# A causal solve of 128 rows per tile: three hops of 32 rows for seven of 16

## The chip, the cores and the metric

The kernel runs on 1 core of a Trainium2 chip. The metric is device time in microseconds (us), measured outside the profile. A profiled execution gives the trace, and has a time of its own.

## The reference, cut to what matters

The whole kernel computes four layers on x[4, 512, 128]: a selective scan, an attention with a mixture of experts, the causal layer below, and attention with experts again. The change touches the causal layer alone (16 heads of 8 columns, 4 sequences of 512 rows):

```python
logits = jnp.einsum('bhqd,bhkd->bhqk', q, k) * scale
probs = jax.nn.softmax(logits + causal_mask, axis=-1)
L = jnp.eye(s, dtype=probs.dtype) - jnp.tril(probs, -1)
rhs = jnp.diagonal(probs, axis1=-2, axis2=-1)[..., None] * v
A = jax.scipy.linalg.solve_triangular(L, rhs, lower=True)
return A.transpose(0, 2, 1, 3).reshape(b, s, HID) @ Wd.T + bd
```

For each head a lower triangular system of 512 rows is solved with 8 right sides. Row i of A needs all the rows before it.

## The kernel before, in words

`delta_phase` (L1459) is the causal layer. It goes over 16 tiles of 128 rows, n = 0 to 15 (4 sequences of 4 tiles), one after the other, since tile n needs the rows solved in the tiles before it in its sequence. A tile's solve has these parts:

- `from_earlier` (L2302) multiplies the solved rows of earlier tiles with the off-diagonal exponentials. With the tile's own right side that gives `g_nat`.
- Before that, POOL inverts the 128 diagonal blocks of 16x16 (8 blocks of rows by 16 heads, one block per partition) in `inverse_block` (L1700): one product with 1/sum (L1704), 28 small products and adds (L1710, L1715), the unit (L1718), a last product (L1722, `xz_blk`).
- SP carries data around for this, in `inverses` (L1776), `blocks_out` (L1757) and `sums_out` (L1767). `blocks_out(n)` writes the 8 diagonal blocks of the exponentials to DRAM with 8 DMAs (L1761), waits for them and loads them as `e_blk`, one block per partition (L1765). `sums_out(n)` does the same for the row sums (L1769, L1774); DVE takes their reciprocal `zi_blk` (L2042), which releases POOL. `inverses(n)` waits for POOL's last step, stores `xz_blk` (L1778), waits, and loads it with 8 DMAs into block-diagonal place, `xT` (L1785).
- PE multiplies exponentials and inverses (`multiplied`, L2244, four groups of 4 heads, 128x128x128 each), and ACT copies the result to `mT` (L1853).
- The solve: `inverse` (L2315) applies the inverses to `g_nat`, and then seven turns of 16 rows, k = 1 to 7, in two halves of 8 heads each: `product` (L2319) of the rows solved so far with `mT`, DVE adds 16 columns to `aT` (L2120), PE transposes `aT` back (L2293, `turned`), and ACT copies it to `a_nat` (L1890). `output` (L2295) multiplies with Wd, and DVE adds to x (L2090).

Every engine runs a program in order, and the order is written out by hand. In iteration n of the outer loop (n = -6 to 15) the turns of tile n are taken, and between them stand 14 places, h = 0 to 13, at which `beside(n, h)` does work for later tiles: at these **hooks** the maxima of tile n+3 or n+4 (up to 2 groups per hook), the scores and exponentials of tile n+3, the sums of tile n+2 (column at h = 3, reciprocal at h = 7), the products for `mT` of tile n+1 (h = 9 to 12, MT_HOOKS). At the start of a sequence the hooks also do its rotation and splitting into bf16 parts (h = 0 to 6 of the iteration four tiles ahead), and SP stores these parts and loads the operands `q_op` and `k_op` (L1740, L1746, L1748; 1152 KB and three times 384 KB). For the first tile of a sequence the scores stand at h = 10 to 13, otherwise from h = 0.

SP's order in iteration n is: `inverses(n+1)`, `blocks_out(n+2)`, `sums_out(n+2)`, `shifts` (maxima, L1750), and where a new sequence comes, the parts and the operands:

```python
if in_program(n + 1):
    inverses(n + 1)
if in_program(n + 2):
    blocks_out(n + 2)
    sums_out(n + 2)
```

So the work of POOL on tile n+2 is released at h = 7 of iteration n, and its result goes to SP at the head of iteration n+1.

## Time and profile before

| what | value |
|---|---|
| median of 3 runs | 1795.72 us (1794.52 to 1796.07) |
| profiled execution, its own time | 1797.81 us |
| its span in the profile | 1795.7 us |
| mean granted TensorE clock | 0.82 |
| PE / DVE / ACT / POOL busy | 74% / 60% / 42% / 31% |
| causal layer in the trace | about 788 to 1388 us |

Busy shares are averages over four layers with different limits. In a timeline row the first number is the start in us from the span's start, the second the time until the last of the merged instructions has ended; SPq is SP's queue, where a duration is that of issuing, not of the transfer. "x16" counts instructions. An fp32 matmul stands as two records (PE) with two weight loads (PEld), a transpose as one. A row of a table of stretches holds its two ends, its length, the busy us and instructions (x) of PE, PEld, DVE, ACT and POOL, then PEclk (the granted TensorE clock, 1 is 2.4 GHz), the DMA share and GB/s. Brackets at a row's end give the engine's idle time before it and what ended it.

### The profile page before, as it was taken

The page shows a single profiled execution, that of the slowest core. Times are in us where ns is not written, and L with a number is a line of the kernel's source. Part 1 is how long each engine was busy: PE and PEld are TensorE (multiplying, and loading weights), DVE is VectorE, ACT ScalarE, POOL GpSimd, SP SyncE. Part 2 cuts the span into 40 slices and gives each one's busy share as a digit, 9 for nine tenths or more (in the row PEclk, how much of TensorE's full clock was granted, in tenths as well). Part 3 has the DMA queues.
Part 4 walks back from the last instruction along what each step waited for, and adds up shares of the span by engine and source line. Part 5 has one row for each costly group of instructions (what it writes and reads, how often), then busy time and mean ns, then how long its engine had stood idle before and what let it go on. Part 6 is the DMA issues. An engine that isn't in the chain of part 4 may idle for free. (4 is left out here: it accounts for less than half of the span.)

```text
span 1795.7 us, 31360 instructions
## 1 busy us (share of the span) xinstructions
PE 1336.6 (74%) x11698; PEld 690.8 (38%) x11698; DVE 1084.9 (60%) x2290; ACT 760.3 (42%) x1622; POOL 559.0 (31%) x782
## 2 busy tenths in 40 slices
PE   2646666655999986733788988988978589999855
PEld 1212222221223222731465666765656212322255
DVE  2789899966878762533645635635512587886143
ACT  2445444420366675521342443433422016566734
POOL 1266556632122111530332422422331321310133
PEclk9659899985699998875687976977977569999968
DMA  8600000003233100213141141141110222410012
GB/s 258 221 0 1 0 0 0 0 3 92 51 102 114 42 9 6 63 37 71 20 86 26 16 90 22 18 88 22 21 21 8 74 72 59 151 49 9 6 48 74
DMA packets 118060, 92.03 MB, mean 51 GB/s; under 512 B 85855, under 2 KB 108959, under 8 KB 116735
## 3 DMA queue, kind: packets, MB, share of 16 engines
q1 hardware_dynamic: 115422, 84.99, 18.9%
q0 software_dynamic: 2496, 5.13, 0.9%
q8 instruction: 91, 1.49, 0.4%
q14 instruction: 51, 0.42, 0.1%
HBM read 69.55 MB, written 38.36 MB: 60 GB/s over the span
## 5 line engine op out<-in xcount | busy, mean ns | idle before, releaser
L980 DVE TENSOR_REDUCE f_row_min<-f_ps 128x1 f32<-128x512 f32 x512 | 335.6, 681 | 113.3 <-PE f_ps L1272 107.5
L874 ACT ACTIVATE f_e<-f_ps 128x512 f32<-128x512 f32 x512 | 289.0, 601 | 219.9 <-PE f_ps L1297 210.3
L1272 PE MATMUL f_ps<-f_operands 72*128 72x512 bf16 x512 | 229.1, 452 | 60.6 <-DMA f_operands<-k_scr 24.0
L1297 PE MATMUL f_ps<-f_operands 75*128 75x512 bf16 x512 | 191.3, 393 | 7.9 <-ACT f_e L874 7.9
L260 POOL TENSOR_TENSOR m_drive<-m_du,m_b_row 128x1024 f32<-128x1024 f32 x64 | 154.2, 2414 | 98.2 <-ACT m_b_row L309 95.5
L1272 PEld LDWEIGHTS f_ps<-f_operands 72*128 72x128 bf16 x512 | 51.8, 102 | 278.8 <-DVE f_row_min L980 221.4
L417 DVE TENSOR_TENSOR_SCAN m_h<-m_ps,m_drive 128x512 f32<-128x512 f32 x128 | 149.1, 1206 | 3.4 <-POOL m_drive L260 3.4
L1981 DVE TENSOR_REDUCE d_row_min<-d_ps 128x1 f32<-128x384 f32 (+3 forms) x176 | 106.3, 634 | 68.0 <-PE d_ps L2186 67.2
L1308 PE MATMUL f_ps<-f_e,f_v_op 128*32 128x512 f32 x1024 | 141.1, 624 | 1.4 <-ACT f_e L874 1.4
L517 PE MATMUL m_ps<-m_hC,sb_ident 128*128 128x512 f32 x256 | 126.0, 615 | 5.6 <-DVE m_hC L426 5.6
L2120 DVE TENSOR_TENSOR d_aT<-d_ps,d_aT 128x16 f32<-128x16 f32 x224 | 37.7, 168 | 140.7 <-PE d_ps L2288 140.4
L1890 ACT COPY d_a_nat<-d_ps 128x64 f32<-128x64 f32 x224 | 47.8, 213 | 165.8 <-PE d_ps L2293 165.1
L494 PE MATMUL m_ps<-m_bc,sb_pick 96*128 (+1 forms) x128 | 50.8, 407 | 88.8 <-DVE m_hC L426 72.4
L2183 PE MATMUL d_ps<-d_k_op,d_q_op 72*128 72x128 bf16 (+3 forms) x256 | 77.7, 377 | 46.9 <-DMA d_k_op<-k_scr 28.0
L2293 PE MATMUL d_ps<-sb_ident,d_aT 128*128 128x128 f32 x256 | 90.1, 354 | 28.9 <-DVE d_aT L2120 26.6
L1704 POOL TENSOR_TENSOR d_xT_blk<-d_e_blk,d_zi_blk 128x256 f32<-128x256 f32 x16 | 13.2, 828 | 256.8 <-DVE d_zi_blk L2042 256.8
L309 ACT COPY m_b_row<-m_ps 128x512 f32<-128x512 f32 x64 | 37.5, 586 | 128.5 <-PE m_ps L494 128.5
L2250 PE MATMUL d_ps<-d_xT,d_e_nat 128*128 128x128 f32 x512 | 89.1, 330 | 1.4 <-ACT d_e_off L1848 1.4
L313 ACT ACTIVATE m_ps<-m_delta,m_A 128x512 f32 x128 | 83.6, 689 | 2.7 <-DVE m_h L417 2.2
L2250 PEld LDWEIGHTS d_ps<-d_xT,d_e_nat 128*128 128x128 f32 x512 | 81.4, 241 | 4.1 <-issue 3.0
L2288 PE MATMUL d_ps<-d_mT,d_a_nat 32*32 32x16 f32 (+6 forms) x3584 | 77.4, 195 | 4.4 <-ACT d_a_nat L1890 3.9
L760 POOL DMA_INDIRECT f_rows_scr<-f_h2n,f_place_u x32 | 32.5, 1015 | 153.8 <-DVE f_place_u L1104 146.4
(250 smaller groups left out, 2407.2 us busy)
## 6 DMA issues: line engine op xcount, KB each, us to landing
f_rows_scr<-blank SPq DMA_DIRECT2D x2, 8707.5 KB, 42.2
f_wall<-f_wall SPq DMA_DIRECT2D x2, 4624.0 KB
f_operands<-q_scr SPq DMA_DIRECT2D x32, 288.0 KB
f_operands<-k_scr SPq DMA_DIRECT2D x96, 96.0 KB
d_q_op<-q_scr SPq DMA_DIRECT2D x4, 1152.0 KB
d_k_op<-k_scr SPq DMA_DIRECT2D x12, 384.0 KB
q_scr<-f_part SPq DMA_DIRECT2D x24, 128.0 KB, 2.3
k_scr<-f_part SPq DMA_DIRECT2D x24, 128.0 KB, 2.4
```

The costliest lines, as they stand in the source:

```text
L260: nc.gpsimd.tensor_tensor(drive[:, n % AHEAD, :, :], du[:, :, now], b_row[:, n % AHEAD, :].unsqueeze(1).to_broadcast([P, HALVES, S]), ALU. ...
L313: last = nc.scalar.activation(ps[:, DECAY + HALVES * (n % 2) + k, :], delta[:, k, now], ACT.Exp, scale=A[:, k, n:n + 1])
L417: last = nc.vector.tensor_tensor_scan(h[:, n % 2, k, :], ps[:, DECAY + HALVES * (n % 2) + k, :], drive[:, n % AHEAD, k, :], 0.0, ALU.mult, ...
L517: last = nc.tensor.matmul(ps[:, Y + k, :], core.ident[:, :], hC[:, n % 2, k, :], start=(n == 0), stop=(n == N_STATE - 1))
L874: nc.scalar.activation(e_sb[:, n % 3, hh, :], ps[:, SCORE[u % SCORE_BANKS], :], ACT.Exp, scale=SCALE).then_inc(s["e_out"], 1)
L980: nc.vector.tensor_reduce(row_min[:, b % 2, u // TPB, u % TPB:u % TPB + 1], ps[:, MAXQ[u % MAX_BANKS], :], AX.X, ALU.max, negate=True).the ...
L1272: nc.tensor.matmul(ps[:, MAXQ[u % MAX_BANKS], :], q_op(b, QK)[:, hd, t * P:(t + 1) * P], k_op(b, QK)[:, hd, :], start=True, stop=True).the ...
L1297: nc.tensor.matmul(ps[:, SCORE[u % SCORE_BANKS], :], k_op(b, QKS)[:, hd, t * P:(t + 1) * P], q_op(b, QKS)[:, hd, :], start=True, stop=True ...
L1308: last = nc.tensor.matmul(ps[hh * HEAD_COLS:(hh + 1) * HEAD_COLS, O_BANK, :], v_of(b, t, g * GROUP + hh), e_sb[:, n % 3, hh, :], start=(t ...
L1981: nc.vector.tensor_reduce(row_min[:, n % 2, g * heads:(g + 1) * heads], dve_bank("maximum", n, g)[:, 0:heads * cols].rearrange("p (h c) -> ...
L2250: last = nc.tensor.matmul(bank[:, hh * P:(hh + 1) * P], e_nat[:, n % 3, hd, :], xT[:, n % 2, hd, :], start=True, stop=True)
L2293: nc.tensor.transpose(turn_bank(half), src[:, half, :], core.ident[:, :]).then_inc(done, 1)
```

## The change

- The solve goes in three hops of 32 rows (HOP, `product`, `turned`, `added`). The sums are transposed back and added in natural order straight into `a_all`; DVE does the adds, ACT copies the products `uT`.
- The inverse of a block of 32 is joined from two of 16 on PE: `paired` at h = 5 (64 matmuls of 32x32x32, 16 heads by 4 blocks), DVE masks, `joined` at h = 7 (64 more), DVE adds: `yT`. `mT` is built from `yT` in three groups at h = 9, 10, 11, of 16 matmuls with 32 rows and 32, 64 or 96 weight columns.
- For this POOL writes the inverses in two orders (one more product of 128x256), and SP loads them with 16 DMAs for 8. `e_blk` has two buffers, and `blocks_out` is done one tile earlier: after `sums_out`, and for the first tile of a sequence as the last thing of SP's iteration.
- The output leaves the solve: POOL packs `a_all` into `a_out` at the head of the next iteration, PE transposes it at h = 1, ACT copies, PE multiplies once at h = 3, DVE adds to x there. The loop has one more iteration.
- Constants: `d_wd` in half the size, `pair_mask` of 32 columns for `off_blocks` of 128, fewer and smaller memsets.

```diff
-HOOKS = 2 * TURNS
+HOP = 32
+HOPS = P // HOP
+LAST_HOP = HOPS - 1
+HOOKS = 14
+PAIR_HOOK, JOIN_HOOK = 5, 7
+TURN_OUT, OUTPUT = 1, 3
-MT_HOOKS = (9, 10, 11, 12)
+MT_HOOKS = (9, 10, 11)
...
             @block.gpsimd
-                nc.gpsimd.memset(xT[:, :, :, :], 0.0).then_inc(s["set"], 1)
+                nc.gpsimd.memset(xp[:, :, :, :, :], 0.0).then_inc(s["set"], 1)
...
-                    nc.gpsimd.tensor_tensor(xz_blk[:, :, :], xT_blk[:, :, :],
+                    nc.gpsimd.tensor_tensor(xz_blk[:, 0, :, :], xT_blk[:, :, :],
                                             zi_blk[:, :].unsqueeze(2).to_broadcast([P, BLK, BLK]),
                                             ALU.mult).then_inc(s["blk_step"], 1)
+                    nc.gpsimd.tensor_tensor(xz_blk[:, 1, :, :], xT_blk[:, :, :].rearrange("p c i -> p i c"),
+                                            zi_blk[:, :].unsqueeze(1).to_broadcast([P, BLK, BLK]),
+                                            ALU.mult).then_inc(s["blk_step"], 1)
+
+                def packed(n):
+                    pool.wait_ge(s["a_sb"], 2 * HOPS * (n + 1))
...
+                    for half in range(2):
+                        nc.gpsimd.tensor_copy(by_group(a_out[:, heads_of(half), :]),
+                                              own_cols(a_all[:, n % TPB, :], half)).then_inc(s["a_packed"], 1)
...
             @block.sync
-                    if n >= 1:
-                        sp.wait_ge(s["blk_step"], BLK_STEPS * (n - 1) + 1)
-                    sp.dma_start(e_blk[:, :, :], e_scr[n].rearrange("k h i j -> (k h) i j")).then_inc(s["e_in"], 16)
+                    if n >= 2:
+                        sp.wait_ge(s["blk_step"], BLK_STEPS * (n - 2) + 1)
+                    sp.dma_start(e_blk[:, n % 2, :, :], e_scr[n].rearrange("k h i j -> (k h) i j")).then_inc(blocks_in(n), 16)
...
                     for k in range(BLKS):
-                        own = slice(k * BLK, (k + 1) * BLK)
-                        sp.dma_start(xT[own, n % 2, :, own], x_scr[n, k].rearrange("h c i -> c h i")).then_inc(s["x_in"], 16)
+                        own, cols = slice(k * BLK, (k + 1) * BLK), slice(k % 2 * BLK, (k % 2 + 1) * BLK)
+                        for form in range(2):
+                            sp.dma_start(xp[own, n % 2, form, :, cols], x_scr[n, k, :, form].rearrange("h r c -> r h c")).then_inc(
+                                s["x_in"], 16)
...
                     if in_program(n + 2):
-                        blocks_out(n + 2)
                         sums_out(n + 2)
+                    if in_program(n + 3) and (n + 3) % TPB:
+                        blocks_out(n + 3)
                     if in_program(n + 3) and (n + 3) % TPB == 0:
                         shifts(n + 3)
...
                     if in_program(n + 4) and (n + 4) % TPB != 0:
                         shifts(n + 4)
+                    if in_program(n + 3) and (n + 3) % TPB == 0:
+                        blocks_out(n + 3)
...
             @block.scalar
+                def hop_out(n, k):
...
+                    own = slice(k * HOP, (k + 1) * HOP)
+                    for half in range(2):
+                        act.wait_ge(s["u_ps"], u_done(n, k, half))
+                        nc.scalar.copy(uT[:, half, own], ps[:, STEP[half], own]).then_inc(s["u_sb"], 1)
...
             @block.vector
+                def paired(n):
+                    dve.wait_ge(s["dve_ps"], in_dve("pair", n))
+                    nc.vector.tensor_tensor(pair[:, :, :], dve_bank("pair", n).rearrange("p (h i) -> p h i", h=NH),
+                                            w["pair_mask"].unsqueeze(1).to_broadcast([P, NH, HOP]), ALU.mult).then_inc(s["dve_out"], 1)
+
+                def joined(n):
+                    dve.wait_ge(s["dve_ps"], in_dve("join", n))
...
+                    nc.vector.tensor_tensor(yT[:, n % 2, :, :], dve_bank("join", n).rearrange("p (h i) -> p h i", h=NH),
+                                            xp[:, n % 2, 0, :, :], ALU.add).then_inc(s["dve_out"], 1)
...
+                for n in range(-LEAD, TILES_N + 1):
...
+                    if in_program(n):
+                        first_rows(n)
+                    for h in range(3, 6):
+                        beside(n, h)
+                    added(n, 1)
+                    for h in range(6, 9):
+                        beside(n, h)
+                    added(n, 2)
...
             @block.tensor
+                def in_blocks(bank, lhs, rhs):
+                    for hd in range(NH):
+                        for b in range(HOPS):
+                            rows = hop_rows(b)
+                            last = nc.tensor.matmul(bank[rows, hd * HOP:(hd + 1) * HOP], lhs(rows, hd), rhs(rows, hd),
+                                                    start=True, stop=True)
+                    last.then_inc(s["dve_ps"], 1)
+
+                def paired(n):
+                    pe.wait_ge(s["x_in"], 16 * 2 * BLKS * (n + 1))
+                    in_blocks(dve_free("pair", n), lambda rows, hd: e_nat[rows, n % 3, hd, rows],
+                              lambda rows, hd: xp[rows, n % 2, 0, hd, :])
...
+                    rows = hop_rows(i + 1)
+                    for hd in range(NH):
+                        last = nc.tensor.matmul(bank[0:(i + 1) * HOP, hd * HOP:(hd + 1) * HOP],
+                                                e_nat[rows, n % 3, hd, 0:(i + 1) * HOP], yT[rows, n % 2, hd, :],
                                                 start=True, stop=True)
...
+                def product(n, k):
...
+                    own, rows = slice(k * HOP, (k + 1) * HOP), slice(0, k * HOP)
+                    pe.wait_ge(s["act_out"], in_act("mt", n, k - 1))
+                    for half in range(2):
+                        pe.wait_ge(s["a_sb"], a_done(n, k - 1, half))
+                        side_by_side(half, a_all[:, n % TPB, :], lambda hd: mT[rows, n % 2, k - 1, hd, :], rows, own, s["u_ps"])
...
+                    beside(n, 4)
+                    product(n, 1)
+                    beside(n, 5)
+                    turned(n, 1)
+                    beside(n, 6)
+                    beside(n, 7)
+                    product(n, 2)
+                    beside(n, 8)
+                    turned(n, 2)
+                    beside(n, 9)
+                    beside(n, 10)
+                    product(n, 3)
+                    beside(n, 11)
+                    turned(n, 3)
```

In `inverse(n)` the 16 matmuls of 128x128 become 64 of 32x32 by 8 columns, all into one bank; DVE copies them to `a_all` (`first_rows`).

## Rows read from the trace of the kernel before

**Rows 1.** Lines L1704, L1722 and the longest wait for a DMA, causal layer.

```profile
L1704 POOL TENSOR_TENSOR d_xT_blk<-d_e_blk,d_zi_blk x16: 822/827/838, 865.8 to 1341.6; 128x256 f32<-128x256 f32 x16
L1722 POOL TENSOR_TENSOR d_xz_blk<-d_xT_blk,d_zi_blk x16: 622/622/625, 877.5 to 1352.9; 128x256 f32<-128x256 f32 x16
DVE d_zi_blk L2042 <- DMA d_z_blk<-z_scr: 41.5, 10, 7.3
```

**Rows 2.** Timeline, 1294 to 1313 us, SP's queue and POOL.

```profile
1294.75 0.62 POOL L1722 TENSOR_TENSOR d_xz_blk<-d_xT_blk,d_zi_blk 128x256 f32<-128x256 f32 x1
1295.40 0.34 SPq L1778 DMA_DIRECT2D x_scr<-d_xz_blk  x1
1297.11 4.50 SPq L1785 DMA_DIRECT2D d_xT<-x_scr  x8
1301.66 3.91 SPq L1761 DMA_DIRECT2D e_scr<-d_e_nat  x8
1307.80 0.34 SPq L1765 DMA_DIRECT2D d_e_blk<-e_scr  x1
1308.18 0.43 SPq L1769 DMA_DIRECT2D z_scr<-d_zT  x1
1310.05 0.34 SPq L1774 DMA_DIRECT2D d_z_blk<-z_scr  x1
1311.93 0.83 POOL L1704 TENSOR_TENSOR d_xT_blk<-d_e_blk,d_zi_blk 128x256 f32<-128x256 f32 x1 [16.56 <-DVE d_zi_blk L2042]
```

**Rows 3.** Stretches from one L1704 to the next: length, engines' busy time, PEclk, DMA.

```profile
894.00:922.00 28.00, 23.24 (x359) 18.28 (x359) 16.49 (x39) 15.57 (x38) 9.69 (x31) 0.74 0.15 22
922.00:959.00 37.00, 30.05 (x485) 21.83 (x485) 13.30 (x43) 6.94 (x25) 9.65 (x31) 0.68 0.49 102
959.00:989.00 30.00, 26.64 (x449) 19.69 (x449) 17.34 (x60) 12.26 (x33) 10.80 (x32) 0.87 0.14 21
989.00:1021.00 32.00, 30.10 (x547) 21.06 (x548) 20.02 (x58) 14.30 (x39) 11.19 (x33) 1.00 0.14 21
1049.00:1088.00 39.00, 31.24 (x485) 22.54 (x485) 13.32 (x43) 7.03 (x26) 9.64 (x31) 0.68 0.47 97
1088.00:1119.00 31.00, 28.12 (x443) 20.54 (x444) 17.40 (x58) 11.90 (x32) 10.70 (x32) 0.78 0.14 21
```

**Rows 4.** Timeline of SP's queue, 1048 to 1080 us: a sequence's operands.

```profile
1055.01 0.88 SPq L1746 DMA_DIRECT2D d_q_op<-q_scr  x1
...
1061.43 0.35 SPq L1778 DMA_DIRECT2D x_scr<-d_xz_blk  x1
1073.25 3.75 SPq L1785 DMA_DIRECT2D d_xT<-x_scr  x8
```

**Rows 5.** Landing of L1785; products on PE; L1942 and L2288 (ns, min/median/max).

```profile
DMA to landing us min/median/max: 1.6/1.9/3.7
...
1005.15 0.31 PE L2288 MATMUL d_ps<-d_mT,d_a_nat 16*32 16x16 f32 x16
...
L1942 DVE TENSOR_TENSOR d_v_raw<-d_ps,sb_rows x4: 691/692/692, 801.7 to 1132.4; 128x512 f32<-128x512 f32 x4
...
L2288 PE MATMUL d_ps<-d_mT,d_a_nat x3584: 177/183/238, 903.5 to 1385.5; 16*32 16x16 f32 x29, 48*32 48x16 f32 x29, 80*32 80x16 f32 x29, 112*32 112x16 f32 x29
...
1024.39 1.06 PE L2250 MATMUL d_ps<-d_xT,d_e_nat 128*128 128x128 f32 x8
```

**Rows 6.** Timeline of ACT, 1093 to 1101 us: the last exponential of tile 8.

```profile
1099.89 0.60 ACT L1843 ACTIVATE d_e_nat<-d_ps 128x512 f32<-128x512 f32 x1 [0.20 <-PE d_ps L2206]
```

**Rows 7.** Timeline of the layer's start: memsets.

```profile
788.28 3.51 POOL L1685 MEMSET d_xT<- 128x4096 f32 x1 [11.68 <-POOLq L2386]
793.66 0.22 DVE L1912 MEMSET d_unit_blk<- 128x1 f32 x16 [3.87 <-POOL d_a_all L1686]
```

**Rows 8.** Timeline of DVE in the last tile: second halves of turns 3 and 4.

```profile
1378.89 0.17 DVE L2120 TENSOR_TENSOR d_aT<-d_ps,d_aT 128x16 f32<-128x16 f32 x1 [0.20 <-PE d_ps L2288]
1380.14 0.17 DVE L2120 TENSOR_TENSOR d_aT<-d_ps,d_aT 128x16 f32<-128x16 f32 x1 [0.20 <-PE d_ps L2288]
```

**Rows 9.** Groups by line, 870 to 1400 us: weight loads of the turns' transposes, idle before.

```profile
L2293 PEld LDWEIGHTS d_ps<-sb_ident,d_aT 128*128 128x128 f32 x256 | 40.0, 156 | 52.0 <-DVE d_aT L2120 35.5 <-DVE d_aT L2114 8.5 <-issue 3.1
```

More of the change, by code:

```diff
@@ L2063, in beside @@
                         maximum(m, g)
+                    if in_program(n + 1) and h == PAIR_HOOK:
+                        paired(n + 1)
+                    if in_program(n + 1) and h == JOIN_HOOK:
+                        joined(n + 1)
                     for m, g in block_sums_in(n, h):
@@ L2123, in _ @@
[L2123 to L2133 removed]
+                        own, target = (by_group(t[:, heads_of(half), :]) for t in (vn[:, n % 4], g_nat))
@@ new lines, in added @@
+                def added(n, k):
+                    if not in_program(n):
+                        return
+                    own = slice(k * HOP, (k + 1) * HOP)
+                    for half in range(2):
+                        target = own_cols(a_all[:, n % TPB, :], half)[own]
+                        dve.wait_ge(s["un_ps"], u_done(n, k, half))
+                        if k == 1:
+                            dve.wait_ge(s["a_sb"], a_done(n, 0, half))
+                        nc.vector.tensor_tensor(target, turned_cols(half)[own], target, ALU.add).then_inc(s["a_sb"], 1)
@@ new lines, in paired, with joined @@
+                def paired(n):
+                    pe.wait_ge(s["x_in"], 16 * 2 * BLKS * (n + 1))
+                    in_blocks(dve_free("pair", n), lambda rows, hd: e_nat[rows, n % 3, hd, rows],
+                              lambda rows, hd: xp[rows, n % 2, 0, hd, :])
+                def joined(n):
+                    pe.wait_ge(s["dve_out"], in_dve("pair", n))
+                    in_blocks(dve_free("join", n), lambda rows, hd: xp[rows, n % 2, 1, hd, :],
+                              lambda rows, hd: pair[rows, hd, :])
@@ L2361, in _, with inverse @@
-                output(TILES_N - 1)
+                def inverse(n):
+                    pe.wait_ge(s["gn_sb"], 2 * (n + 1))
+                    pe.wait_ge(s["dve_out"], in_dve("join", n))
+                    for hd in range(NH):
+                        for b in range(HOPS):
+                            rows = hop_rows(b)
+                            last = nc.tensor.matmul(a0_bank()[rows, hd * HD:(hd + 1) * HD], yT[rows, n % 2, hd, :],
+                                                    g_nat[rows, hd, :], start=True, stop=True)
+                    last.then_inc(s["a0_ps"], 1)
```

306 lines of the change are left out of this document (160 added, 146 removed).

## The prediction

> **What bounds the kernel now.** The page's busy shares say nothing about the causal layer, so I first read its lines. POOL starts a tile's inverses 16 times, from 865.8 to 1341.6 us [rows 1]: 15 intervals, 31.7 us in the mean. The list of waits then tells what that start waits for: POOL always for DVE's reciprocal, and DVE in 10 of 16 cases for the DMA that brings the sums, for 41.5 us together [rows 1]. A DMA that a fast engine waits for again and again is the end of a chain, so I followed one on SP's queue [rows 2]. POOL ends a tile at 1295.37; SP stores its result and waits until 1297.11 (1.74 us), issues 8 loads (4.50), 8 stores of the next tile's blocks, waits for them and loads them (6.5 from 1301.66 to 1308.18), sends the sums there and back (1.87, then 1.88 until POOL starts). That is 16.56 us. POOL itself takes 12.0 (1341.6 to the end of the last L1722 at 1353.5 [rows 1]). The ring POOL, SP, POOL has 28.5 us, and intervals of 28 us stand in the table of stretches [rows 3]. **It is a ring of one POOL and one SP queue, not the seven turns, that paces most tiles.** PE is busy for 23 of those 28 us.
>
> The long intervals confirm it. In those of 37 to 39 us (three) the DMA share is 0.47 to 0.49 [rows 3]: a sequence's operands are issued at 1055.01, and the small store behind them, issued at 1061.43, lets SP go on at 1073.25 only [rows 4]. Only where PE is busy for 30.1 of 32 us at full clock (989 to 1021 [rows 3]) does PE pace; I count three such intervals.
>
> **What the change does to that ring.** Each interval is the longest of three paths; I price the two that it touches.
>
> POOL: one more product of 128x256. The two such products take 0.62 and 0.83 [rows 1]; it reads transposed, as the 0.83 does, so POOL takes 12.8.
>
> SP: 16 loads for 8. Eight took 4.50 and 3.75 [rows 2, 4], so 16 take 7.5 to 9.0; I take 8.7, since these stretches come now and then. The last lands 1.9 after its issue [rows 5]. From POOL's end to the inverses in place: 1.74 + 8.7 - 0.45 + 1.9 = 11.9 us.
>
> The sums no longer stand behind the blocks: 1.74 + 8.7 + 1.87 + 1.88 = 14.2 for 16.56. With POOL that path is 27.0, 1.5 less than now.
>
> But `paired` waits on PE for those loads at h = 5, while the products for `mT` waited at h = 9 to 12. Behind it on PE stand hooks 5 to 13, and DVE behind PE, with the reciprocal of h = 7 that starts POOL. That closes a **second ring**: POOL 12.8, SP 11.9, and from there to h = 7. The pair: a small product of 16 records takes 0.31 [rows 5], of which 0.18 is one record's own time (the median of L2288 [rows 5]), so about 0.13 for 16 starts, 0.032 for four records on four groups of columns. 128 records are 32 such rounds, 1.0 us, and 1.2 with the tail. DVE's mask from PSUM: 0.69, as L1942 of that shape [rows 5]. Two adds of 64 columns, 0.45. That and the signals make 2.8 us until POOL starts. With two maxima of 0.7 at h = 6: 4.2. Where a sequence's split stands at h = 5 and 6 (two subtractions of 1024 columns, and ACT's cast between them): 6.1. I have no row for the split as a whole; 5 to 7 bounds it, three times. The ring is 27.5, 28.9 or 30.8.
>
> **The 15 intervals.**
> - The first: 28.9 for 28, +1.
> - Three with the split (as 894 to 922, two of 28 and one of 30 [rows 3]): 30.8 for 28.9, +6 together.
> - Three with operands: SP reaches them 4.3 later (8 more loads), POOL's start has moved by 1.5 (18.0 for 16.56 after its end), so 2.8 later against it; behind the landed store 8.7 - 0.45 + 1.9 + 4.2 = 14.4 follows for 15.1 before (1073.25 to 1088.4). +2.1 each, +6.
> - Three behind a new sequence's first scores (as 959 to 989 and 1088 to 1119 [rows 3]): here `blocks_out` of that tile is now SP's last step, and waits for exponentials at h = 13, with the next `inverses` queued behind. The last ended at 1100.49 [rows 6], 12.1 after POOL's start at 1088.4, so POOL's result, ready at 12.8, waits until 12.1 + 6.5 = 18.6. Then 11.9 and 4.2: 34.7 for 30.6. +4.1 each, +12.
> - Three that PE paces: 0. PE's work grows and shrinks alike: pair, join and the 64 small matmuls of `inverse` are 3 x 1.0 where `inverse` was 0.9; `mT` has 96 records with 32, 64 or 96 weight columns. Eight records of L2250 with 128 weight columns take 1.06 [rows 5], of which about 0.27 is the last one's tail, so 0.11 each; by weight columns, 32 records each of 96, 64 and 32 take 2.7 + 1.8 + 0.9 = 5.4 for 3.6 (32 of 128). Against this 16 transposes fall to 6 and 14 products to 6; a pair with its gaps is some 0.4, -3.9 together.
> - The last two, without maxima: 27.5 for 29, -3.
>
> Sum: **+22 us**. From the last start of POOL to the layer's end: inverses in place 5.0 later; then pair and join with their DVE steps (4.0) and longer `mT` (1.8) against turns that no longer stand between (-2.7); then four turns fewer in the last tile, 1.25 each (1378.89 to 1380.14 [rows 8]), and small steps, -5.3 with the longer way out over POOL in it. +2.8. At the start, DVE waits 3.87 us for POOL's memsets; that of 4096 columns, 3.51 us, becomes half [rows 7]: -1.8.
>
> Costed at nothing: ACT has 10 copies fewer and one more per tile, and is not last anywhere in [rows 2]. The output's packing on POOL stands before the next tile's inverses, in 16 us of idle time [rows 2]; if that cover went it would be 0.6 per tile. DVE's adds fall from 14 to 6, but pair and join are two of 0.69: even. Smaller constants: 0.1 MB of the first load, at most 0.4 us.
>
> Total 22.3 + 2.8 - 1.8 = +23.3 on an execution of 1797.8 us (span 1795.7), 2.1 above the median of the runs. On that median: 1795.7 + 23.3 = **1819 us**.
>
> **A price the trace doesn't hold.** In this trace no product of the causal layer has rows that begin above partition 0; the four column groups of L2288 run side by side, 16 records in 0.31 us [rows 5]. `in_blocks` puts four row groups after each other, into one bank. If those ran one after the other, 128 records would take 4.1 instead of 1.0; if they overlap more, nothing is gained on the ring beyond 1 us. I take 1.0, the row that is nearest. The Trainium skill (TensorEngine Tiling (Array Packing), Restrictions and Gotchas) says that different row tiles cannot access the same PSUM bank simultaneously; by that rule the first of the two holds, and the sum would be that of rival 1. No run here shows it yet.
>
> **Rivals.**
> 1. Row groups take turns (13%). Pair +3.1 on the second ring in 12 intervals, 37 us, and three times 3.1 in the tail: +46, **1865 us**. For it: nothing in the trace. Against it: the column groups overlap.
> 2. The turns pace, not the ring (18%): **faster**. If the inverses land before PE comes to h = 5, `paired` waits for nothing, and what counts are round trips. PE's weight loads stood idle for 52.0 us ahead of the turns' transposes [rows 9]; four of seven turns gone saves 30: **1766 us**. Place: PE at h = 5; it decides where PE's way from h = 7 to the next h = 5 is over 24.7 us. For it: PE is busy for 30 us in several stretches. Against: only 23 of 28 in others, and the 41.5 us of waits for the sums.
> 3. The second ring at its lower bounds (10%): 16 loads in 7.5 and 1 us less from pair to h = 7 take 2.2 from each of 11 intervals, 24 us: **1795 us**, no change.
> The change could also fail to shorten the solve at all; that is in the forecast already, since hops are not on the ring.
>
> **How the numbers follow.** The forecast has 59%. About 0.2% (3.6 us) is what a measurement of this kernel can tell from no change. Rival 2 lies below that, rival 3 on both sides of it. Faster 0.21, same 0.05, slower 0.74. The range reaches from just above rival 2 to just above rival 1, 1770 to 1872; the forecast's own, by its bounds (7.5 to 9.0, 5 to 7, exponentials 2 us earlier or later), is 1800 to 1840.
>
> **What would show it.** PE idle ahead of `paired`, ended by the DMA into `xp`, 2 to 5 us in most tiles; starts of L1704's successor 27 to 31 us apart, 34 to 35 three times, 39 to 42 three times; DVE's reciprocal no longer waiting for its DMA. `paired` and `joined` 1.2 us long at full clock, over 4 if rival 1 holds. I am wrong if PE shows no idle time there, or if the ordinary intervals fall below 27 us.

## The result, and the profile after

The changed kernel takes **1935.88 us** in the median of 4 runs (1935.27 to 1948.57); the kernel before took 1795.88 (4 runs) beside it. The ratio is 1.0798, 95% interval 1.0754 to 1.0843: slower by 140 us, where +23 was forecast. The sign was right, the size was six times too small, and the range given was 1770 to 1872.

The profiled execution has a span of 1934.1 us for 1795.7, and the 138 us between them all lie in the causal layer. From the first start of POOL's product to the layer's last addition it took 522 us and takes 660. The stretch over the whole layer, first of the kernel before, then of the changed one (columns as in [rows 3]: length, busy time of PE, PEld, DVE, ACT, POOL, granted clock, DMA):

```profile
866.00:1388.00 522.00, 444.05 (x7611) 326.18 (x7609) 243.08 (x740) 190.05 (x543) 160.74 (x501) 0.81 0.21 37
```

```profile
866.00:1527.00 661.00, 558.32 (x12045) 449.61 (x12043) 259.56 (x645) 153.56 (x384) 178.37 (x549) 0.64 0.21 36
```

PE's busy time rose by 114 us, and it runs 12045 matmul records for 7611; the forecast had PE's work even. The granted clock fell from 0.81 to 0.64 of full speed, which the forecast did not ask about.

POOL's chain and the way of the sums are what the forecast said: POOL's last product takes 0.83 us, for 0.62 [rows 1], and DVE's reciprocal no longer waits for its DMA (41.5 us before [rows 1], 0.6 now). The lines of the changed kernel, then its list of waits in the layer:

```profile
L1731 POOL TENSOR_TENSOR d_xT_blk<-d_e_blk,d_zi_blk x16: 821/823/846, 866.2 to 1464.7; 128x256 f32<-128x256 f32 x16
L1752 POOL TENSOR_TENSOR d_xz_blk<-d_xT_blk,d_zi_blk x16: 822/826/844, 878.3 to 1476.6; 128x256 f32<-128x256 f32 x16
```

```profile
POOL d_xT_blk L1731 <- DVE d_zi_blk L2098: 263.5, 16, 26.9
ACT d_mT L1898 <- PE d_ps L2361: 185.2, 48, 11.1
...
PE d_ps L2342 <- DMA d_xp<-x_scr: 25.6, 9, 5.2
...
PE d_ps L2418 <- issue: 14.4, 9, 2.4
PE d_ps L2342 <- issue: 12.2, 8, 2.8
...
DVE d_zi_blk L2098 <- DMA d_z_blk<-z_scr: 0.6, 1, 0.6
```

POOL, which starts a tile, now waits 263.5 us for DVE, DVE waits for PE, and ACT waits 185.2 us for the products of `mT` (L2361). PE waits for the inverses (L2342 is the matmul of pair and join) in 9 of 16 tiles only. So PE paces most tiles, not the second ring. Two rows "issue" are new: PE idle inside its own streams, for nothing that the profile shows.

The stretches between two starts of POOL that answer to [rows 3]:

```profile
895.00:927.00 32.00, 30.15 (x667) 25.02 (x669) 17.54 (x35) 11.20 (x25) 9.95 (x32) 0.61 0.21 31
927.00:968.00 41.00, 33.27 (x767) 27.79 (x760) 14.05 (x38) 6.89 (x20) 10.82 (x35) 0.62 0.46 96
968.00:1016.00 48.00, 39.10 (x746) 30.38 (x743) 18.79 (x54) 10.39 (x24) 11.95 (x36) 0.57 0.15 22
1016.00:1061.00 45.00, 39.69 (x819) 30.73 (x818) 22.22 (x52) 11.88 (x28) 12.30 (x36) 0.73 0.15 22
```

The third was 30 us long with PE busy for 26.6 at clock 0.87, the fourth 32 at full clock. PE's timeline in one tile shows where its time went:

```profile
1067.52 1.91 PE L2361 MATMUL d_ps<-d_yT,d_e_nat 32*32 32x32 f32 x32
1069.67 3.62 PE L2361 MATMUL d_ps<-d_yT,d_e_nat 32*64 32x32 f32 x32
1073.81 5.32 PE L2361 MATMUL d_ps<-d_yT,d_e_nat 32*96 32x32 f32 x32
1091.28 1.93 PE L2342 MATMUL d_ps<-d_xp,d_e_nat 32*32 32x32 f32 x128
```

`mT` takes 1.91 + 3.62 + 5.32 = **10.85 us** in every tile; the forecast had 5.4. The pair's 128 records take 1.93 us in most tiles, at a granted clock of 0.5 (1.2 GHz), and 1.29 in the few that fall in a time of full clock, as the last tile's join:

```profile
1429.00 1.93 PE L2342 MATMUL d_ps<-d_xp,d_e_nat 32*32 32x32 f32 x128
1433.10 1.29 PE L2342 MATMUL d_ps<-d_pair,d_xp 32*32 32x32 f32 x128
```

The forecast had 1.2 (1.0 and a tail), and 4.1 in place of the 1.0 if the row groups took turns. They run side by side, and rival 1 is false. The Trainium skill (TensorEngine Tiling (Array Packing), Restrictions and Gotchas) says that different row tiles cannot access the same PSUM bank simultaneously. Here four of them write one bank at once, each into partitions of its own, at 1.29 us / 128 = 10 ns per record; the measurement decides.

Last, SP's queue behind a new sequence's first scores. POOL's last product starts at 979.82 and takes 0.82:

```profile
978.65 0.69 SPq L1795 DMA_DIRECT2D d_q_op<-md_scr  x1
991.68 3.74 SPq L1801 DMA_DIRECT2D e_scr<-d_e_nat  x8
996.67 0.34 SPq L1805 DMA_DIRECT2D d_e_blk<-e_scr  x1
997.05 0.43 SPq L1818 DMA_DIRECT2D x_scr<-d_xz_blk  x1
```

POOL's result is stored 16.4 us after its end; the forecast had 5.8, by the same mechanism, since the exponentials that SP waits for came 12.1 us after POOL's start and now come 24.

### The profile page after: what moved, and what is told of

Its sections match the earlier page's. It is cut to its first block and busy times, and to the rows that moved or that the text cites. A ratio compares the mean times of both kernels' runs of the same rounds, so it can differ in the third digit from the quotient of the medians.

```text
span 1934.1 us, 40328 instructions
## 1 busy us (share of the span) xinstructions
PE 1451.3 (75%) x16130; PEld 814.1 (42%) x16130; DVE 1099.9 (57%) x2193; ACT 723.3 (37%) x1462; POOL 574.3 (30%) x830
## 5 line engine op out<-in xcount | busy, mean ns | idle before, releaser
L2361 PE MATMUL d_ps<-d_yT,d_e_nat 32*32 32x32 f32 (+2 forms) x1536 | 173.3, 290 | 1.6 <-ACT d_e_off L1892 1.1
L2361 PEld LDWEIGHTS d_ps<-d_yT,d_e_nat 32*32 32x32 f32 (+2 forms) x1536 | 167.3, 215 | 11.1 <-issue 6.6
L2274 PE MATMUL d_ps<-d_k_op,d_q_op 72*128 72x128 bf16 (+3 forms) x256 | 82.6, 395 | 38.9 <-DMA d_k_op<-k_scr 28.8
L2202 DVE TENSOR_TENSOR d_a_all<-d_ps,d_a_all 32x64 f32<-32x64 f32 x96 | 19.1, 220 | 146.7 <-PE d_ps L2423 145.7
L1898 ACT COPY d_mT<-d_ps 32x512 f32<-32x512 f32 (+2 forms) x48 | 27.7, 578 | 185.2 <-PE d_ps L2361 185.2
L1731 POOL TENSOR_TENSOR d_xT_blk<-d_e_blk,d_zi_blk 128x256 f32<-128x256 f32 x16 | 13.2, 827 | 263.5 <-DVE d_zi_blk L2098 263.5
L426 DVE TENSOR_TENSOR m_hC<-m_h,m_ps 128x1024 f32<-128x1024 f32 x64 | 78.1, 1221 | 2.1
L494 PEld LDWEIGHTS m_ps<-m_bc,sb_pick 96*128 96x128 bf16 x128 | 12.5, 100 | 150.8 <-DVE m_hC L426 115.6
```

Of the source, the lines that this page charges most:

```text
L2274: nc.tensor.matmul(bank[:, hh * cols:(hh + 1) * cols], q_op[0:QK_ROWS, hd, rows_of(t)], k_op[0:QK_ROWS, hd, 0:cols], start=(hh == 0), stop ...
L2361: last = nc.tensor.matmul(bank[0:(i + 1) * HOP, hd * HOP:(hd + 1) * HOP], e_nat[rows, n % 3, hd, 0:(i + 1) * HOP], yT[rows, n % 2, hd, :], ...
```

## The experiments

All in one table first; the intervals are means over the kind of tile that the forecast priced, between starts of POOL's first product, with the tail from the last start to the layer's end.

| us | first | 3 split | 3 operands | 3 late blocks | 3 PE-paced | last 2 | tail | whole kernel |
|---|---|---|---|---|---|---|---|---|
| before | 28.3 | 29.0 | 37.9 | 30.6 | 32.3 | 29.1 | 46.1 | 1795.9 |
| forecast | 28.9 | 30.8 | 40.0 | 34.7 | 32.3 | 27.5 | 48.9 | 1819 |
| changed | 28.4 | 35.7 | 40.9 | 47.8 | 43.5 | 33.2 | 61.3 | 1935.9 |
| e1_cols | 28.3 | 35.0 | 42.3 | 40.9 | 38.3 | 30.7 | 56.0 | 1887.5 |
| e13_few_codes | 28.4 | 32.8 | 38.4 | 38.9 | 35.6 | 28.8 | 48.7 | 1848.6 |
| e17_few_hooks | 26.6 | 28.4 | 39.5 | 34.1 | 33.4 | 28.0 | 48.5 | 1813.5 |

Times below are medians of 4 runs (one for e2_k128), ratios are to the kernel before on the same chip in the same job. The intervals are those of one profiled execution each. In these the layer, from POOL's first start to the last addition, takes 522 us before, 660 changed, 615 in e1_cols, 572 in e13_few_codes and 537 in e17_few_hooks. What lies before and behind it took 1268 to 1282 us over all the profiled executions, and most of that spread lies behind the layer, where no edit reaches. So a difference of some 10 us between two whole kernels tells little of the layer, and where it matters the layer's own time stands beside it.

### The price of mT

**e1_cols**: the weights of each `mT` matmul are split into pieces of 32 columns, one per column group.

```diff
-    last = nc.tensor.matmul(bank[0:(i + 1) * HOP, ...], e_nat[rows, n % 3, hd, 0:(i + 1) * HOP], yT[...])
+    for j in range(i + 1):
+        last = nc.tensor.matmul(bank[hop_rows(j), ...], e_nat[rows, n % 3, hd, hop_rows(j)], yT[...])
```

> The products for mT with 64 and 96 weight columns are split into pieces of 32 columns, each in its own column group (96 logical matmuls per tile instead of 48, the same result). Theory A (PE paces: the mT stream takes 1.91 + 3.62 + 5.32 = 10.85 us per tile because every record stands alone in the array and the clock is at 1.2 GHz there): the three groups fall to about 1.9 each or less, 5.1 us or more saved in each of 16 tiles, so about 1854 us or below. Theory B (waits for the inverses and SP's order made the loss, PE's length is covered): less than 20 us gained, 1915 or more.

Measured: 1887.47 us, ratio 1.0523 (1.0481 to 1.0564), between the two theories. `mT`'s busy time fell from 173.3 us to 90.3 for the 16 tiles, 5.6 per tile, the forecast's price; 48 us came back.

**e2_k128**: each `mT` matmul contracts over all 128 rows (its values differ), the weight columns stay.

```diff
-    e_nat[rows, n % 3, hd, 0:(i + 1) * HOP], yT[rows, n % 2, hd, :],
+    e_nat[:, n % 3, hd, 0:(i + 1) * HOP], yT[:, n % 2, hd, :],
```

> The products for mT contract over all 128 rows instead of 32; number, weight columns and moving columns stay (the sums then hold foreign rows, so the output is another). If the narrow contraction makes a record slow, the spacing of records falls from 53/107/160 ns to 28/56/84 at the same clock. If it is the weight columns at 1.2 GHz, the spacing stays 53/107/160 wherever the clock is at that level. Whether the clock rises with more rows at work is open: if it does, 28/56/84 and a granted clock near 1, and about 1850 us.

Measured: 1909.48 us (one run). A record's time does not depend on the number of rows; it does on the columns and the clock. Four of the 16 groups of 96 columns ran at full clock here, none in the changed kernel; `mT` is busy for 157 us in place of 173, and the run is 26 us shorter. Why the clock rose for them is not shown. PE in this run:

```profile
982.33 5.27 PE L2361 MATMUL d_ps<-d_yT,d_e_nat 128*96 128x32 f32 x32
...
1150.07 2.86 PE L2361 MATMUL d_ps<-d_yT,d_e_nat 128*96 128x32 f32 x32
```

**The forecast's 2.7 for that group was right for the full clock**, and it had the full clock from the one row that it used: L2250's eight records at 1024.39 took 1.06 us [rows 5], in two microseconds of granted clock 1.00. The same eight took 1.91 at 926.84, at clock 0.50. The kernel before, PE's timeline and then the two stretches:

```profile
926.84 1.91 PE L2250 MATMUL d_ps<-d_xT,d_e_nat 128*128 128x128 f32 x8
```

```profile
1024.00:1026.00 2.00, 2.00 (x45) 1.76 (x42) 1.86 (x8) 1.21 (x4) 1.61 (x6) 1.00 0.00 0
...
926.00:929.00 3.00, 3.00 (x36) 2.41 (x39) 0.17 (x1) 1.00 (x3) 2.37 (x9) 0.50 0.33 76
```

A run that left out the products of `mT` for all heads but the last, e3_no_mt, gave no time. e5_mt_wide keeps the time of the products and takes away most of their number.

**e5_mt_wide**: one matmul of 512 moving columns per group, with the first head's exponentials for all heads (so its values differ).

```diff
-    for hd in range(NH): last = nc.tensor.matmul(bank[..., hd * HOP:(hd + 1) * HOP], e_nat[rows, n % 3, hd, ...], yT[..., hd, :])
+    last = nc.tensor.matmul(bank[...], e_nat[rows, n % 3, 0, ...], yT[rows, n % 2, :, :])
```

> Each group of mT is one matmul of 512 moving columns in place of 16 of 32 (its values differ, everything else is kept). The three groups should take 3 us or less per tile for 10.85. If mT is the term that made PE the bound (theory A), about 8 us go from each of 13 to 14 tiles that PE paces, until the second ring or SP paces: 1805 to 1845 us, about what the forecast said of the rings (1819), and the granted clock of the layer comes back from 0.57-0.74 to 0.75 or more. If the other small matmuls (pair, join, products of 32 rows) hold clock and tiles down by themselves (theory B), it stays above 1860 us with a clock still near 0.6.

Measured: 1886.87 us, 1.0498 (1.0464 to 1.0531). I had expected 2.6 us per tile; the records took 1.08 us each, 5.9 per tile, and the clock stayed low (0.62 in the layer), so this is e1_cols over again in another form: with `mT` at its forecast price the kernel takes **1887, not 1819**. `mT` is 48 to 49 us of the miss, and 68 are left.

### SP's order, and PE's wait

**e4_blocks** moves `blocks_out` of a sequence's first tile from the end of SP's step to the place ahead of `sums_out`.

```diff
+    if in_program(n + 2) and (n + 2) % TPB == 0:
+        blocks_out(n + 2)
     if in_program(n + 2):
         sums_out(n + 2)
...
-    if in_program(n + 3) and (n + 3) % TPB == 0:
-        blocks_out(n + 3)
```

> The blocks of a sequence's first tile go out one iteration later, after the inverses and before the sums, so that SP's queue does not stand behind the exponentials of h = 13 (before: the store of the inverses stood 16 to 18 us after POOL's end, three times). Theory A (PE paces): less than 12 us gained. Theory B: 30 us or more, since three intervals lose 10 us and more each.

Measured: 1915.23 us, 1.0668 (1.0622 to 1.0714), 20 us less than the changed kernel, between the two theories; in the layer it is 13 us, 647 for 660.

**e6_cols_blocks**: both edits.

> The edits of e1_cols (1887.5 us) and e4_blocks (20 us less than the changed kernel) together. Theory A (PE paces most tiles, SP's late blocks_out delays POOL in three of them, by 10 us there in e1_cols): between half and all of e4's gain remains, 1866 to 1878 us. Theory B (SP's lateness and PE's length overlap): no gain on e1_cols, 1884 us or more.

Measured: 1884.92 us, 1.0511 (1.0475 to 1.0547): 3 us off e1_cols, inside the intervals. In the layer it is 10 us, 605 for 615; the rest of the profiled kernel was 10 us longer there. SP's store is on time (1.5 us after POOL's end at most, up to 10.9 in e1_cols). PE waits for the inverses in 6 tiles only, 19.8 us together; in the others it still comes late to the pair.

**e7_hooks**: e6_cols_blocks with the pair behind the reciprocal that it held up.

```diff
-PAIR_HOOK, JOIN_HOOK = 5, 7
+PAIR_HOOK, JOIN_HOOK = 8, 9
-MT_HOOKS = (9, 10, 11)
+MT_HOOKS = (10, 11, 12)
```

> e6_cols_blocks with the pair at h = 8, the join at h = 9 and mT at 10 to 12, so that PE's wait for the inverses no longer stands ahead of the reciprocal of h = 7. If the second ring of the forecast paces (theory B), PE's waits ahead of the pair go and it is 15 us or more faster than e6_cols_blocks. If PE paces (theory A): within 6 us of it.

Measured: 1870.85 us, 1.0405 (1.0373 to 1.0437). 14 us less than e6_cols_blocks (11 in the layer, 594 for 605), just under theory B's 15: the second ring is there, and small.

**e10_diag_hooks** stands on e7_hooks and groups `mT`'s six blocks by their distance from the diagonal, two groups at a time in two banks, so that five blocks run side by side. ACT then copies six pieces per tile for three, and the first hop waits for all of `mT`.

```diff
-    for hd in range(NH):
-        for j in range(i + 1): last = nc.tensor.matmul(bank[hop_rows(j), ...], e_nat[rows, n % 3, hd, hop_rows(j)], ...)
+    banks = {step: act_free("mt", n, step) for step in steps}
+    for hd in range(NH):
+        for step in steps:
+            for b in range(step, LAST_HOP):
+                rows, cols = hop_rows(b + 1), hop_rows(b - step)
+                last[step] = nc.tensor.matmul(banks[step][cols, ...], e_nat[rows, n % 3, hd, cols], yT[rows, ...], ...)
```

> e7_hooks (1870.9 us) with mT's six blocks grouped by their distance from the diagonal, so that blocks of different row groups and column groups run side by side, five of them at once in two banks: 3.8 us per tile for 5.6. If PE still paces the tiles (theory A): 12 to 25 us less than e7_hooks. If the rings do (theory B): within 6 us of it.

Measured: 1875.53 us, 1.0444 (1.0394 to 1.0493), no gain on e7_hooks. PE's busy time fell, from 475 to 450 us in the layer, and yet nothing came of it. ACT's copies have a part in that (PE waits 14.5 us for them inside `mT`). The rest pointed to a cause that I had not priced. PE in a tile of e10_diag_hooks:

```profile
1007.77 0.82 PE L2348 MATMUL d_ps<-d_pair,d_xp 32*32 32x32 f32 x43
1010.87 0.74 PE L2348 MATMUL d_ps<-d_pair,d_xp 32*32 32x32 f32 x36 [2.27 <-issue]
1011.54 0.38 PE L2288 MATMUL d_ps<-sb_ident,d_row_min 128*16 128x128 f32 x1
1012.41 1.21 PE L2373 MATMUL d_ps<-d_yT,d_e_nat 32*32 32x32 f32 x90 [0.48 <-DVE d_yT L2116]
1014.71 1.00 PE L2373 MATMUL d_ps<-d_yT,d_e_nat 32*32 32x32 f32 x70 [1.08 <-issue]
```

In the middle of the join's matmuls, which wait for nothing, PE stands still for 2.27 us, then again inside `mT`. PE's "issue" rows in the list of waits add up to 73 us in the layer here, to 46 in e7_hooks, 5 in the kernel before, 29 in the changed one and 38 in e1_cols. The list of DMA queues has one for instructions. Its row for the layer, of the kernel before, of the changed one and of this run (packets, MB, share of the 16 engines):

```profile
q8 instruction: 60, 0.98, 0.8%
```

```profile
q8 instruction: 95, 1.56, 1.0%
```

```profile
q8 instruction: 107, 1.75, 1.2%
```

The packets' own times tie the two together. In the layers of the changed kernel, e1_cols, e5_mt_wide, e10_diag_hooks and e9_before_streams (below), PE stood idle by "issue" for over 1 us 93 times. Each of the 93 times it went on 1.2 to 1.75 us after a packet of q8 had ended; of all instants of these layers, some 9 to 13% lie so behind a packet. So PE uses up its small instructions faster than the next packets come. The next two runs ask what that costs.

### Code

**e9_before_streams**: the kernel *before*, with 64 matmuls of 32x32 ahead of each of a tile's four groups of `mT`, overwritten by them.

```diff
     bank = act_free("mt", n, i)
+    for hd in range(NH):
+        for b in range(4):
+            nc.tensor.matmul(bank[rows, hd * 32:(hd + 1) * 32], e_nat[rows, n % 3, hd, rows], xT[rows, n % 2, hd, rows], ...)
```

> The kernel before, with 64 matmuls of 32x32x32 (as one pair) ahead of each of a tile's four groups for mT, overwritten by them: 4 x 1.29 us per tile at full clock, 7.7 at half. Theory A (a layer with more small matmuls is granted less clock, and that slows everything else on PE too): the layer's granted clock falls from 0.80 to 0.74 or less, PE's busy time rises by clearly more than 16 x 5.2 = 83 us, and the time goes up by 50 us or more. Theory B (the low clock of the changed kernel comes from its waits, not from its small matmuls): the clock stays within 0.03 of 0.80, and with some 4 us of slack per tile in the ordinary intervals the time rises by 35 us or less.

Measured: 1924.19 us, 1.0706 (1.0625 to 1.0786), +128 us. The groups of PE in the layer:

```profile
L2251 PE MATMUL d_ps<-d_xT,d_e_nat 32*32 32x32 f32 x8192 | 104.1, 207 | 51.6 <-issue 50.2 <-ACT d_e_off L1848 1.4
L2255 PE MATMUL d_ps<-d_xT,d_e_nat 128*128 128x128 f32 x512 | 92.7, 336 | 3.2 <-issue 3.2
```

The time rose as theory A had it, but not for its reason: the layer's clock went *up*, to 0.84. The streams cost 104 us of their own, and 50 more of "issue" stand ahead of them, with 124 packets of instructions in the layer. So small matmuls did not lower the clock of this kernel, and with the rests they cost half as much again as their busy time.

**e13_few_codes**: e5_mt_wide with pair, join and inverse as 4 matmuls each, with the first head's weights on all heads' columns, in place of 64 (values differ).

```diff
-    for hd in range(NH):
-        for b in range(HOPS):
-            last = nc.tensor.matmul(bank[rows, hd * HOP:(hd + 1) * HOP], lhs(rows, hd), rhs(rows, hd), ...)
+    for b in range(HOPS):
+        last = nc.tensor.matmul(bank[rows, :], lhs(rows, 0), rhs(rows, slice(0, NH)), ...)
```

> e5_mt_wide (1886.9 us) with pair, join and inverse each as 4 matmuls of 32 weight columns on all heads' columns in place of 64 small ones (values differ). PE's own time stays about what it was (a 512-column record took 1.08 us there, four side by side, so some 2.2 us for 1.9 at half clock), but 720 of PE's some 1330 records per tile go, and with them the code that has to be fetched. Theory C (PE runs out of code in the streams of small matmuls: idle stretches of 1 to 3 us that wait for nothing but a code fetch): 1822 to 1850 us, and PE's idle time by 'issue' in the layer falls from some 30 us to under 8. Theory A (clock and busy time alone): within 12 us of 1887.

Measured: 1848.58 us, 1.0275 (1.0215 to 1.0336), **38 us less than e5_mt_wide** (43 in the layer). At half clock a pair or join takes 1.93 us in both, with 8 records here and 128 there. The packets of instructions fell from 84 to 39, and the list of waits has no "issue" left on PE, for 25 us. But the code is not the whole of the 38 us: PE's busy time in the layer fell too, from 490 to 451 us. 16 of these are the inverse, which has 8 records per tile here and 128 there, and the granted clock is 0.66 for 0.62. So the 38 us are what fewer instructions bring in all; how they divide between rests, the inverse and the clock isn't shown. A join of e5_mt_wide, one of e13_few_codes, the inverse in the same two, and the waits of e13_few_codes:

```profile
1053.67 1.93 PE L2342 MATMUL d_ps<-d_pair,d_xp 32*32 32x32 f32 x128 [0.25 <-DVE d_row_min L2037]
```

```profile
1074.54 1.93 PE L2341 MATMUL d_ps<-d_pair,d_xp 32*32 32x512 f32 x8
```

```profile
L2442 PE MATMUL d_ps<-d_g_nat,d_yT 32*32 32x8 f32 x2048 | 23.2, 179 | 9.8 <-issue 5.1 <-DVE d_g_nat L2182 4.7
```

```profile
L2439 PE MATMUL d_ps<-d_g_nat,d_yT 32*32 32x128 f32 x128 | 7.4, 305 | 4.8 <-DVE d_g_nat L2182 4.8
```

```profile
PE d_ps L2341 <- DMA d_xp<-x_scr: 49.9, 12, 9.4
PE d_ps L2274 <- DMA d_k_op<-k_scr: 18.9, 3, 7.5
PE d_ps L2294 <- DMA d_q_op<-md_scr: 7.7, 4, 3.5
```

What comes in place of the rests is the forecast's ring: PE waits for the inverses in 12 tiles, 49.9 us.

**e16_few_blocks** and **e17_few_hooks** put e4's and then e7's edit on it.

> e13_few_codes (1848.6 us) with blocks_out of a sequence's first tile ahead of sums_out. There SP stores POOL's result 9.0, 10.6 and 6.8 us after POOL's end in the three intervals behind a new sequence's first scores. If the queue and the rings pace now (theory A): 15 to 27 us less, 1822 to 1834 us. If PE still paces those tiles, as it did in e1_cols (theory B): 6 us or less.

> e16_few_blocks with the pair at h = 8, the join at 9, mT at 10 to 12, so that PE's wait for the inverses (49.9 us in e13_few_codes) no longer stands ahead of the reciprocal of h = 7. If the forecast's second ring paces (theory A): 15 to 40 us less than e16_few_blocks, near the kernel before. If PE's own work paces (theory B): within 6 us of it.

Measured: 1827.43 us, 1.0201 (1.0150 to 1.0253), and 1813.49 us, 1.0114 (1.0061 to 1.0167). SP's order is worth 21 us where PE does not hide it (19 in the layer; the intervals of the two ratios overlap, and e13_few_codes was on another chip), the second ring 14 (16 in the layer), a little under what I expected. What is left above the kernel before is 22 us.

### The clock

**e8_fill**: e6_cols_blocks with four idle bf16 matmuls of 128x128 on 512 columns ahead of each of pair, join and the groups of `mT`, overwritten by them. **e12_hook_fill**: one each, on e7_hooks. **e11_diag_fill**: two each, on e10_diag_hooks. **e18_few_fill**: ten, ahead of the pair's wait, on e16_few_blocks.

```diff
+    def filled(bank, times):
+        for j in range(times):
+            nc.tensor.matmul(bank, w["ident_b"], w["mask_diag4"], start=True, stop=True)
+        return bank
```

> e6_cols_blocks with 20 idle bf16 matmuls of 128x128 on 512 columns per tile ahead of the small ones (pair, join, mT; four each), overwritten by them. They cost 20 x 0.21 us at full clock, 4.3 us per tile, 8.5 at half. If streams of small matmuls let the granted clock fall (theory A), the clock rises above 0.7 in most stretches and the time stays within +40 us of e6_cols_blocks or falls below it. If the clock is low for another cause (theory B), it stays near 0.6 and the time is 90 to 130 us above e6_cols_blocks.

> e7_hooks (1870.9 us) with one idle bf16 matmul of 512 columns ahead of each of pair, join and the groups of mT: 1.1 us per tile at full clock, 17 us for 16 tiles. Theory A: the clock rises by a few hundredths, and the time is within 8 us of e7_hooks. Theory B: clock unmoved, 17 to 30 us more.

> e10_diag_hooks with two idle bf16 matmuls of 512 columns ahead of each of pair, join and the groups of mT, 2.1 us per tile at full clock, 34 us for 16 tiles. Theory A (the granted clock follows what PE runs, and gives back what the fill costs): granted clock of the layer above 0.68, time within 12 us of e10_diag_hooks. Theory B (clock unmoved): 34 to 60 us more.

> e16_few_blocks with 10 idle bf16 matmuls of 512 columns ahead of the pair's wait for its DMA, 2.1 us per tile at full clock, 4.3 at half, where PE stood idle for 1.3 to 6.4 us in 12 of 16 tiles. If the granted clock follows what PE runs and is a cost of its own (theory A): clock of the layer up by 0.05 or more and time from 15 us below to 8 us above e16_few_blocks. If not (theory B): 10 to 35 us more.

| run | clock of the layer, without and with fill | time, without and with |
|---|---|---|
| e8_fill | 0.65, 0.77 | 1884.9, 1903.8 |
| e12_hook_fill | 0.65, 0.67 | 1870.9, 1870.8 |
| e11_diag_fill | 0.67, 0.71 | 1875.5, 1892.5 |
| e18_few_fill | 0.67, 0.75 | 1827.4, 1837.0 |

Neither theory holds whole. The clock rose in all four, as theory A had it, and e8_fill and e12_hook_fill lie inside its range of time; e11_diag_fill (17 us more) and e18_few_fill (10) lie between the two theories. The clock follows what PE runs, and the slow clock has a price. Of e8_fill's layer:

```profile
L2240 PE MATMUL d_ps<-sb_mask_diag,sb_ident_b 128*128 128x512 bf16 x259 | 92.8, 483 | 44.1 <-DMA d_xp<-x_scr 17.1 <-DVE d_row_min L2037 16.9 <-issue 5.5
L2368 PE MATMUL d_ps<-d_yT,d_e_nat 32*32 32x32 f32 x3072 | 68.1, 204 | 14.1 <-issue 14.1
```

PE is busy for 502.1 us there, 92.8 of them with the fill; the rest, 409.3, took 477.6 in e6_cols_blocks. The same work became 68 us shorter. (The list has 259 of 320 matmuls of the fill, so the fill itself takes somewhat more than 92.8.) But the fill costs more than it gives back in three of the four runs, and nothing changes in the fourth.

**e14_dense** takes the other way, from the changed kernel: `yT` block-diagonal as in the kernel before, `mT` and the inverse as 16 matmuls of 128 rows and 128 weight columns each. **e15_dense_hooks** adds the edits of e4 and e7.

```diff
-    last = nc.tensor.matmul(bank[0:(i + 1) * HOP, ...], e_nat[rows, n % 3, hd, 0:(i + 1) * HOP], yT[rows, n % 2, hd, :], ...)
+    last = nc.tensor.matmul(bank[:, hh * P:(hh + 1) * P], e_nat[:, n % 3, hd, :], yT[:, 0, hd, :], ...)
...
-    last = nc.tensor.matmul(a0_bank()[rows, ...], yT[rows, n % 2, hd, :], g_nat[rows, hd, :], ...)
+    last = nc.tensor.matmul(a0_bank()[:, hd * HD:(hd + 1) * HD], yT[:, 0, hd, :], g_nat[:, hd, :], ...)
```

> The changed kernel with mT and the inverse in the form that the kernel before has: yT laid out block-diagonally, one matmul of 128 rows and 128 weight columns per head for mT (16 for 48) and one per head for the inverse (16 for 64). mT takes 5.6 us per tile for 10.85, PE has 320 records fewer per tile, and the dense matmuls are back in the layer. By mT's time alone (theory A without clock and code): as e1_cols, 1880 to 1895 us. With the code that is saved (theory C) and the clock that the dense matmuls bring: 1840 to 1872 us, granted clock of the layer above 0.70.

> e14_dense with the edits of e4_blocks (blocks_out of a sequence's first tile not last on SP) and e7_hooks (pair at h = 8, join at 9, mT at 10 to 13). Where PE no longer paces all tiles, SP's lateness and the second ring count again: 15 to 40 us less than e14_dense, 1805 to 1850 us. If PE still paces: within 10 us of it.

Measured: 1907.05 us, 1.0642 (1.0599 to 1.0684), and 1919.69 us, 1.0704 (1.0625 to 1.0783). Both expectations failed. The groups of e14_dense, `mT` and the inverse, then the inverse of the kernel before:

```profile
L2365 PE MATMUL d_ps<-d_yT,d_e_nat 128*128 128x128 f32 x512 | 101.0, 365 | 4.9 <-DVE d_yT L2112 3.9 <-ACT d_e_off L1893 0.6
L2445 PE MATMUL d_ps<-d_g_nat,d_yT 128*128 128x8 f32 x512 | 80.0, 297 | 4.8 <-DVE d_g_nat L2186 4.8
```

```profile
L2288 PE MATMUL d_ps<-d_xT,d_g_nat 128*32 128x128 f32 x512 | 17.3, 275 | 5.2 <-DVE d_g_nat L2108 4.4 <-DVE d_g_nat L2098 0.7
```

`mT` took 101.0 us for 173.3, but the inverse 80.0 for 20.8, for its weights have four times the columns, and DVE needs four additions of 0.69 us for one. The kernel before has its inverse the other way round: `g_nat` gives 32 weight columns and the inverse is what moves, 17.3 us. So what I took for its form was not its form, and a kernel with dense `mT` and that inverse was not run. The clock came to 0.67 only. Dense matmuls in the layer are thus not all that the kernel before has for its 0.81, and what else lets the clock fall I cannot say.

## Why the prediction was wrong in size

Of the chain of reasons the following held. The ring of POOL and SP is as described, POOL takes 12.8, the loads land 9 to 11 us after the first of them is issued, for 10.2. The first interval is 28.4 for 28.9. Intervals with operands came to 40.9 for 40.0 in the mean. Pair and join cost 1.29 us at full clock and row groups do not take turns (rival 1). The sums no longer wait. Rivals 2 and 3 are out by the sign.

**The step that failed is "Three that PE paces: 0".** It balanced PE's work at one price, that of full clock, and let PE pace three tiles. PE's balance over the 16 tiles, by the forecast and by the traces, each record's time counted up to the start of the next one:

| us in the layer | forecast | measured |
|---|---|---|
| `mT` | +29 | +89 |
| pair, join and the inverse | +34 | +61 |
| hops that go (transposes and products) | -62 | -77 |
| all other work on PE | 0 | +42 |
| sum | 0 | +114 |

Three terms of it failed:

- **`mT`, 5.4 us per tile, is 10.85.** The row for its price was taken at full clock; all 16 tiles ran at half. By itself 48 us (e1_cols, e5_mt_wide).
- **Small matmuls: their clock mis-sized, their number costed at nothing.** Pair, join and inverse were 1.0 us each and take 1.93, 1.93 and 1.25 in most tiles, at half clock. They are 64 matmuls each, and every fp32 matmul of the trace is two weight loads and two matmul records; PE's records rose from 7611 to 12045, and 28.6 us of rests stand between them, for 5.2 before. With few instructions in their place a kernel without `mT`'s excess is 38 us shorter (e5_mt_wide to e13_few_codes), the rests and the inverse's time included.
- **The clock, costed at nothing.** It fell from 0.81 to 0.64, and the work that both kernels have alike takes PE 42 us more. The largest part of it is `from_earlier`, before and after:

```profile
L2309 PE MATMUL d_ps<-d_e_off,d_a_all 128*32 128x128 f32 x768 | 23.5, 274 | 0.0
```

```profile
L2432 PE MATMUL d_ps<-d_e_off,d_a_all 128*32 128x128 f32 x768 | 37.6, 376 | 0.8
```

"-3.9 together" from the hops that go is not what failed: they save 4.8 per tile. How much of the time the clock makes isn't separated from the other two, since both were at half clock themselves: part of those 48 and 38 us is the clock.

With these PE paces the tiles, and this explains the rest: the exponentials come later, so **late `blocks_out`**, priced +12, cost 20 (e4_blocks), and the **tail**, priced +2.8, cost 15. Of those 20 us the layer's own time shows 13. Where `mT`'s time and the number of instructions are taken away, in e13_few_codes, the forecast's own terms come near their size: the tail is 48.7 for 48.9, the intervals with operands 38.4 for 40.0; SP's order is 21 us for 12, and the second ring, +7 in the first and the split intervals, is 14. The steps from the changed kernel down (e5, e13, e16, e17) are 49, 38, 21 and 14 us, and 22 are left over of 144, against the 1791.3 of the kernel before in that last job. (By the layer's time in the profiles the steps are 45, 43, 19 and 16 us, and 15 are left.) The 22 aren't split further; the PE-paced tiles (33.4 for 32.3) and the clock (0.71 for 0.81) are in them.

The signs that I had written down tell where the forecast held. PE idle ahead of `paired` for the DMA, "2 to 5 us in most tiles", came true in 9 of 16, 25.6 us together, 5.2 at the longest. In the other seven PE came later than the inverses, so there it was PE that paced, and the ordinary intervals were 28 to 38 us for 27 to 31.

**Open**: the cause of the lower clock, and whether any form of this solve beats the kernel before. The best one in which nothing is left out or changed, e7_hooks, is 4% slower, and was not pursued. Its 27000 records, weight loads and matmuls together, would have to become fewer without more weight columns.

## What to carry to other kernels

Price matmuls at both levels of the clock, and ask which level the new stretch will get: the rows of before tell it only for the work that was there. Count PE's instructions beside its time: in e9_before_streams many small matmuls cost half their busy time again in rests that no busy share shows. And where an engine was busy for 23 to 30 of 30 us, "even" on that engine needs the same care as the ring that paces.

## What was unexpected of the hardware

- PE stands still inside a stream of 32x32 matmuls for 1 to 3 us, in e9_before_streams up to 7.1, waiting for nothing that the profile names. All 93 rests over 1 us that were looked at ended 1.2 to 1.75 us after a packet of instructions. The more packets in the layer, the more of them, though not in proportion: with 39, 60, 84, 95, 107 and 124 packets PE has 0, 5, 25, 29, 38 to 73 and 70 us of "issue".
- The time of fp32 matmuls with 32 moving columns goes by their weight columns: 32 records took 1.91, 3.62 and 5.32 us for 32, 64 and 96 of them at 1.2 GHz, and 2.86 for 96 at 2.4 GHz; the number of rows (32 or 128) changed nothing: 5.27 for 5.32.
- Four row groups, each with a column group of its own, run side by side into one bank: 128 records in 1.29 us at 2.4 GHz, 1.93 at 1.2.
- The granted clock rises from 0.65 to 0.77 when bf16 matmuls that compute nothing are put between small ones, and the rest of PE's work shrinks by 68 of 478 us.
